# In odd steps of a recurrence, the state update and the slot's next row become one VectorE operation over 128 columns

## The reference, cut to what matters

```
xn     = layernorm(x)
x_norm = layernorm(xn) * g + b;  x_norm += conv(x_norm, 3 taps over time)
gate, input_gate = x_norm @ gate_w.T + gate_b        # 512 and 512 columns
Bm     = x_norm * sigmoid(input_gate) @ B_w.T + B_b  # 64 columns
Cm     = x_norm @ C_w.T + C_b                        # 64 columns
A_bar  = expm(dt_A * A)                              # 64 x 64
state  = 0
for t in range(2048):                                # the recurrence
    state = layernorm(state @ A_bar + Bm[:, t])      # 8 rows (batch) of 64
    y[:, t] = Cm[:, t] * state
s      = (y @ D_w.T + D_b) * sigmoid(gate)
out    = x + s * silu(xn @ (W + C V_r').T + b)
```

## Time and profile before

| | us |
|---|---|
| median of 3 runs | 2489.87 (2488.64 to 2490.12) |
| the profiled execution's own time | 2491.04 |
| its span, first to last instruction | 2489.2 |
| PE busy | 2448.6 (98%) |
| DVE busy | 2189.7 (88%) |
| POOL busy | 1242.5 (50%) |
| ACT busy | 1013.5 (41%) |

### The profile page before, as it was taken

How to read it: one execution, slowest core, us unless ns; L and a number is a source line. 1 busy time by engine, 2 the same in 40 slices (tenths; PEclk the granted TensorE clock), 3 DMA queues, 4 the chain that set the end, 5 groups by cost and what they waited for, 6 DMA issues and landing times.

```text
span 2489.2 us, 42423 instructions
## 1 busy us (share of the span) xinstructions
PE 2448.6 (98%) x10031; PEld 1307.4 (53%) x10031; DVE 2189.7 (88%) x10934; ACT 1013.5 (41%) x1859; POOL 1242.5 (50%) x2433
## 2 busy tenths in 40 slices
PE   8999999999999999999999999999999999999996
PEld 4555555555555555555555555555555555555544
DVE  6788889988889988889988899888899888899887
ACT  5444333444433444434443434443344444334310
POOL 2444555545555545555545555445555455555443
PEclk9999999999999999999999999999999999999998
DMA  3112211212212122112122112122112122121121
GB/s 113 24 47 56 60 41 41 52 47 60 57 33 52 48 52 60 45 39 58 49 52 60 43 41 55 48 56 60 38 44 52 47 60 53 36 53 48 35 59 36
DMA packets 99678, 125.14 MB, mean 50 GB/s; under 512 B 31975, under 2 KB 48743, under 8 KB 99432
## 3 DMA queue, kind: packets, MB, share of 16 engines
q1 hardware_dynamic: 98560, 121.12, 20.2%
q10 hardware_dynamic: 872, 1.31, 0.2%
HBM read 71.96 MB, written 33.55 MB: 42 GB/s over the span
## 4 chain that ended last, share of the span: by engine, by line
POOL 33%; PE 33%; DVE 24%; issue 9%; ACT 1%; DMA 0%; POOLq 0%; SPq 0%; DVEq 0%; ACTq 0%
POOL dw L429 30%; DVE wq L942 10%; PE bank L1256 7%; DVE dw L969 7%; DVE dw L955 7%; PE bank L1235 6%; PE bank L1245 5%; PE bank L1323 4%; POOL ln L456 3%; PE bank L1324 3%; PE bank L1266 2%; PE bank L1284 1%; PE bank L1275 1%; PE bank L1186 1%; PE bank L1193 1%
## 5 line engine op out<-in xcount | busy, mean ns | idle before, releaser
L429 POOL TENSOR_TENSOR dw<-q,minus_half 8x1 f32<-8x1 f32 x2048 | 1088.0, 531 | 1187.0 <-DVE wq L942 1153.8
L1323 PEld LDWEIGHTS bank<-Mscan,wT 128*65 128x65 f32 x2046 | 225.7, 136 | 623.9 <-issue 614.5
L1245 PE MATMUL bank<-xnorm,gateT 128*128 128x512 f32 x1024 | 506.2, 593 | 0.9 <-DVE sgT L895 0.9
L942 DVE SCALAR_TENSOR_TENSOR wq<-dw 8x65 f32<-8x65 f32 x2048 | 443.6, 217 | 70.2
L1256 PE MATMUL bank<-xnorm,gateT 128*128 128x512 f32 x1024 | 500.7, 595 | 0.1
L1235 PE MATMUL bank<-xnT,WT 128*128 128x512 f32 x1024 | 494.5, 593 | 0.0
L1323 PE MATMUL bank<-Mscan,wT 128*65 128x128 f32 x2046 | 404.0, 279 | 16.0 <-DVE wT L972 12.6
L1324 PE MATMUL bank<-Mscan,wT 128*65 128x128 f32 x2046 | 391.5, 273 | 0.0
L969 DVE SCALAR_TENSOR_TENSOR dw<-dw 8x64 f32<-8x64 f32 x1024 | 280.2, 274 | 113.1 <-POOL dw L429 87.8
L959 DVE SCALAR_TENSOR_TENSOR dw<-bank,dw 8x128 f32<-8x128 f32 x1024 | 342.9, 335 | 6.7 <-PE bank L1324 5.3
L955 DVE SCALAR_TENSOR_TENSOR dw<-dw 8x64 f32<-8x64 f32 x1024 | 279.9, 273 | 77.1 <-POOL dw L429 75.5
(11 more groups left out here) (188 smaller groups left out, 2742.8 us busy)
## 6 DMA issues: line engine op xcount, KB each, us to landing
xc<-in_x SPq DMA_DIRECT2D x252, 128.0 KB, 2.8
xa<-in_x SPq DMA_DIRECT2D x252, 128.0 KB, 2.7
out<-o SPq DMA_DIRECT2D x248, 128.0 KB, 2.4
dw<-dtok SPq DMA_DIRECT2D x127, 96.0 KB
wtok<-dw SPq DMA_DIRECT2D x128, 33.0 KB
gateT<-in_gateT SPq DMA_DIRECT2D x1, 2048.0 KB
WT<-in_WT SPq DMA_DIRECT2D x1, 1024.0 KB, 7.6
xa<-in_x SPq DMA_DIRECT2D x4, 256.0 KB
```

The costliest lines, as they stand in the source:

```text
L429: nc.gpsimd.tensor_tensor(dw[0:B, t, CR:CR + 1], q[:], minus_half[0:B, 0:1], ALU.pow).then_inc(s["r_ready"], 1)
L942: V.scalar_tensor_tensor(out=wq[:], in0=w_eps, scalar=1.0 / S, in1=w_eps, op0=ALU.mult, op1=ALU.mult, accum_out=q[:]).then_inc(s["q_ready" ...
L1245: ins = mm(mbank["gate", m][:], gateT[:, k, P * m:P * m + P], xnorm[p][:, k, :], start=(k == 0), stop=(k == KH - 1))
L1323: mm(scanP[0:WIDE, 0:2 * S], wT[:, 0:WIDE], Mscan[:, 0, :], start=True, stop=False)
```

## The change

The odd step's two updates of 64 columns become one of 128 columns. It takes w(t) and the next row of slot t together: both are scaled by the same r(t-1), and both their sources lie side by side in slot t-1 (columns CM:SLOT). The operation stands where L969 stood, ahead of `square_sum` and the transpose, and signals `w_ready`. The wait for the next quarter's rows comes ahead of it. The semaphore `a_ready` is dropped, and the even step waits for `w_ready` in its place.

```diff
@@ even_step @@
                 wait_for(dve, "r_ready", CT, i, t)
-                wait_for(dve, "a_ready", PAIRS, i, t // 2)
+                wait_for(dve, "w_ready", CT, i, t)
                 V.scalar_tensor_tensor(out=dw[0:B, t, CD:CM], in0=dw[0:B, before, CM:CM2], scalar=r,
                                        in1=dw[0:B, t, CD:CM], op0=ALU.mult, op1=ALU.add).then_inc(s["w_ready"], 1)
@@ odd_step @@
                 r = dw[0:B, before, CR:CR + 1]
-                V.scalar_tensor_tensor(out=dw[0:B, t, CD:CM], in0=dw[0:B, before, CM:CM2], scalar=r,
-                                       in1=dw[0:B, t, CD:CM], op0=ALU.mult, op1=ALU.add).then_inc(s["w_ready"], 1)
-                square_sum(i, t)
-                V.transpose(wT[0:32, 0:S], dw[:, t, CD:CM]).then_inc(s["wT_ready"], 1)
                 if t % QT == QT - 1:
                     of, q = divmod(i * NQ + t // QT + 1, NQ)
                     if of < NC:
                         wait_for(dve, D_IN[q], 16, of, 16)
-                V.scalar_tensor_tensor(out=dw[0:B, t, CM:CM2], in0=dw[0:B, before, CM2:SLOT], scalar=r,
-                                       in1=dw[0:B, t, CM:CM2], op0=ALU.mult, op1=ALU.add).then_inc(s["a_ready"], 1)
+                V.scalar_tensor_tensor(out=dw[0:B, t, CD:CM2], in0=dw[0:B, before, CM:SLOT], scalar=r,
+                                       in1=dw[0:B, t, CD:CM2], op0=ALU.mult, op1=ALU.add).then_inc(s["w_ready"], 1)
+                square_sum(i, t)
+                V.transpose(wT[0:32, 0:S], dw[:, t, CD:CM]).then_inc(s["wT_ready"], 1)
```

More of the change, by code:

```diff
@@ L197, in build @@
             hmean_done hvar_done b0_mm dT0_done dfirst_mm dfirst_done q0_mm q0_done
-            p_ready r_ready w_ready q_ready wT_ready rest_ready a_ready
+            p_ready r_ready w_ready q_ready wT_ready rest_ready
             stats_done mv_done mean_done var_done ln_done z_done zfill y_done halo_y t1_done conv_half xnorm_done xn_done xfill xnT_done
```

## The result

The change made the kernel slower: 2555.94 us (median of 4 runs, 2554.89 to 2556.75) against 2489.26 us on the same chip (4 runs, 2488.07 to 2490.12). The ratio is 1.0269, with a 95% interval of 1.0256 to 1.0282. The difference of 66.7 us stands beside a forecast of 66.9. The profiled execution took 2556.75 us, its span is 2555.0.

The account below looks back on a forecast made before the run. The recurrence's DVE-POOL round trip was taken as the bound; the odd update's 66 ns, 1024 times, gave 67.6 us, less 0.7 for PE waits: 66.9 on 2489.87, so 2557, range 2543 to 2587.

Parts of the forecast that it names:

- The recurrence's round trip sets the time: Update, square sum, POOL's power, next update: 1.18 us a step, taken 2048 times, with all other work fitting beside it.
- The two slopes: Fused update's added cost from 128 and 256 column rows: 65 ns by tensor_tensor, 67 by scalar_tensor_tensor; 66 ns was taken.
- The upper bound of 95 ns: Most the odd update's 64 added columns could cost, from L977: 335 - 240; at that price 97.3 us, 2587.
- The lower bound, 57: Least added ns for the widened odd update: L959 over the 64 column update, less 4 ns for its PSUM source.
- L977's removal is worth 0: The odd step's 240 ns operation behind the transpose lay under POOL's power, so dropping it 1024 times gains 0 on the path.
- POOL's power varies by little, taken as 0: Correction for POOL's power no longer running beside L977: at most -5 ns a time or -5 us, taken as 0.
- The moved wait and the moved transpose cost 0: Quarter wait about 0.6 us earlier but met long before; transpose 66 ns later, as is the L959 needing its product: cost 0.
- The ten pairs in which L959 waits for PE hide up to 0.7 us: Correction: where L959 waited for PE, the 66 ns may vanish in that wait, up to -0.7 us.
- The rival of PE's pace: PE sets the pace for part of the span, so a third of the cost hides: 45 us, 2535; chance 5%.
- The rival of free width: The fused update takes 274 to 279 ns, so the time stays between 2489.9 and 2494.9; chance 4%.
- The pair of rows at 64x64: L1039 217 and L1018 213 ns: a PSUM source costs 4 ns, preferred over the skill's 62 cycles.
- PE's clock: Rival: PE's idle time lowers its clock in the recurrence, costing some hundreds of us; chance 2%.

## Why the prediction was right, point by point

- *The total.* The mechanism is right, but that 66.9 met 66.7 so closely is in part luck. From the first to the last start of L955 the recurrence grew from 2416.4 to 2480.5 us, by 64.1. The profiled execution came to 65.8 because its recurrence began 1.2 us later and the tail was 0.5 longer, which the change does not explain, and the medians add another 0.9.
- *The recurrence's round trip sets the time.* Shown by removal (the next row left out: 2488.74), by addition (an operation behind the transpose: 2557.09) and by dose (33, 67 and 137 us for 32, 64 and 128 columns).
- *The fused update lasts about 340 ns.* It lasts 340. The two slopes over 128 to 256 columns carried over to 64 to 128, but only because all pieces in the kernel before stood behind like instructions: read in the changed kernel, L840's new mean gives (454 - 335)/128 x 64 = 60 ns. The upper bound of 95 ns, against L977, was far off, because L977's 240 ns were those of an operation behind a transpose; the same operation behind the update lasted 266. The lower bound, 57, was off by about 10.
- *L977's removal is worth 0.* It was worth 3.2 ns a pair, some 3 us. The sum's step "worth on the path: 0" was too small by that. Its working took the piece L860 with 0.41 us, which ended about when r came, and not L840 and L847 with 0.47 and 0.46, which ended after it. The later start of the recurrence (58.7 against 57.5, the first start of L955) hid part of it; within the medians the two can't be told apart.
- *POOL's power varies by little, taken as 0.* It took 1085.8 us in all in place of 1088.0, 2.2 less, within the 5 allowed.
- *The moved wait and the moved transpose cost 0.* Right: in the changed kernel the odd steps at the quarters' ends last 1.24 us like the others, and the undoing of the move gained nothing.
- *The ten pairs in which L959 waits for PE hide up to 0.7 us.* Not tested. L959 waited 12 times, 5.5 us.
- *The rival of PE's pace.* A third of the cost should have hidden behind PE. The pair grew by 62.9 ns of the update's 66.9, and nearly all of the gap is accounted for without PE; L959's waits went from 5.3 us in all to 5.5.
- *DVE's busy time falls by 178 us.* It fell from 2189.7 to 2085.7, by 104. The step that failed is the use of an instruction's length for its occupancy: L977 lasted 0.240, but the next instruction started 0.17 behind it, and overlapping time counts once. 1024 x (0.168 - 0.066) = 104.
- *The even updates wait for POOL in nearly all 1024 cases.* The list shows 763, since it leaves out short idle stretches such as the 0.11 us at 1002.55. By the starts in the trace 1018 of 1023 even updates begin 33 to 36 ns behind the end of POOL's power, so the prediction was right.
- *The rival of free width*, from the surcharge that the Trainium skill ("VectorE: DVE Perf Modes", section on the TRN2 errata) puts on a PSUM source. The all-SBUF form lasts 340 ns and the one with a PSUM source 335. The two also differ in what stands ahead of them, but the surcharge would be 65 ns (an estimate from the page's cycles), and no run here shows it. The pair of rows at 64x64 was the better guide.
- *PE's clock* stayed at 1.00 in the recurrence of the changed kernel, from 138 to 2460. PE was busy for 2295.97 of these 2322 us, 98.9% where it had been 99.8%.

## What to carry to other kernels

Fusing two operations saves an engine's time but makes the consumer of the first half wait for the second; where a serial chain sets the pace, ask of every operation whether it stands ahead of the chain's next link, and not how many there are. In such a chain an operation that nothing on the chain needs yet belongs behind the last link, under the other engine's work, even if it costs an instruction more. And here a period that was equal in steps with and without other work told the chain from a full engine, where the shares of busy time did not: PE at 98% and DVE at 88% were both not the bound. Last, a price read from another row held here only where like instructions stood ahead of both.

## What the runs showed of the hardware that was not expected

- With three semaphores to wait for, an instruction's wait can land on a separate semaphore instruction ahead of it. When the last to be met is there, the start comes 0.10 us behind its releaser instead of 0.03 to 0.04. In an even update that is 0.065 us a time, and it made one experiment look like a loss of 3 us by itself (2492.21 against 2488.74).
- An instruction directly behind the transpose is 26 to 33 ns shorter than the same one elsewhere. L840 takes 0.44 us at 1002.00, behind the transpose, and 0.47 at 1003.28, behind L959, and its mean fell from 470 to 454 ns with the fusion. The next row's operation takes 240 ns behind the transpose and 266 behind another update. That the instruction ahead reads its scalar from memory is not the reason: L925, which has no scalar, takes 271 ns on average behind another L925 and 239 behind the transpose. What makes the difference was not tested.
- POOL's power on 8x1 took 530 ns on average in one kernel and 532 in another with the same POOL program, over all 2048. With two of them on each pair's path this is 3.7 ns a pair, as much as L977 cost.

All L925 of the changed kernel, min/median/max ns; the shortest are those behind the transpose:

```profile
L925 DVE TENSOR_TENSOR xg<-bank,G x16: 239/268/293, 2525.0 to 2549.2; 128x128 f32<-128x128 f32 x16
```
